# Wide attention of a decoder: one half of every rotated head copied in place, the other half moved by 4 transfers per tile

## The reference

```python
q = split_heads(x @ Wq); k = split_heads(x @ Wk); v = split_heads(x @ Wv)
x1, x2 = (x[..., 0::2], x[..., 1::2])     # apply_rope, on q and k
rot = jnp.stack([x1 * cos - x2 * sin, x1 * sin + x2 * cos], axis=-1)
sim = jnp.einsum('bid,bjd->bij', q, k) * scale
attn = jax.nn.softmax(jnp.where(causal[None], sim, -jnp.inf), axis=-1)
out = jnp.einsum('bij,bjd->bid', attn, v)
return out @ Wo + bo
```

## Time and profile before

| | |
|---|---|
| median of 3 runs | 1898.75 us (1895.04 to 1898.91) |
| profiled execution | 1897.24 us, span 1895.4 us |
| granted TensorE clock, mean | 0.944 of full speed |
| PE busy in the span | 1635.5 us, 86% |
| DVE | 1480.9 us, 78% |
| POOL | 1401.5 us, 74% |
| ACT | 960.2 us, 51% |
| transfers from `wa_rot` to `wa_whole` | 1024 of 64.0 KB |

### The profile page before, as it was taken

How to read it: one execution, slowest core, us unless ns; L and a number is a source line. 1 busy time by engine, 2 the same in 40 slices (tenths; PEclk the granted TensorE clock), 3 DMA queues, 4 the chain that set the end, 5 groups by cost and what they waited for, 6 DMA issues and landing times. The chain is left out here.

```text
span 1895.4 us, 63438 instructions
## 1 busy us (share of the span) xinstructions
PE 1635.5 (86%) x24719; PEld 1351.4 (71%) x24719; DVE 1480.9 (78%) x3166; ACT 960.2 (51%) x2012; POOL 1401.5 (74%) x1249
## 2 busy tenths in 40 slices
PE   4999999999998927489999999999999868918886
PEld 2677777777776826367778778888888657918775
DVE  6888888888887682488899988888888665688765
ACT  3677777777776332344454444444443453125554
POOL 3777778877777545498899888888888635857776
PEclk9999999999999857699999999999999978959999
DMA  8000023000000041344444333343434226552222
GB/s 250 14 7 9 6 73 125 16 18 15 15 16 7 1 134 36 107 117 108 120 119 106 93 96 96 97 97 97 97 97 97 69 73 193 177 164 81 75 76 56
DMA packets 155071, 154.03 MB, mean 81 GB/s; under 512 B 37246, under 2 KB 106944, under 8 KB 154160
## 3 DMA queue, kind: packets, MB, share of 16 engines
q1 hardware_dynamic: 140528, 130.91, 25.6%
q0 software_dynamic: 6704, 15.61, 2.8%
q10 hardware_dynamic: 7696, 5.71, 1.1%
HBM read 58.77 MB, written 26.71 MB: 45 GB/s over the span
## 5 line engine op out<-in xcount | busy, mean ns | idle before, releaser
L1424 POOL TENSOR_TENSOR wa_rot<-wa_rot,wa_cross 128x1024 f32<-128x1024 f32 x128 | 309.1, 2415 | 46.3 <-DVE wa_cross L1636 44.6
L412 POOL TENSOR_TENSOR sa_sd<-sa_sd,sa_mx 128x1024 f32<-128x1024 f32 x128 | 243.3, 1901 | 133.6 <-DVE sa_mx L648 133.6
L592 ACT ACTIVATE sa_sd<-sa_sd 128x1024 f32<-128x1024 f32 x128 | 135.5, 1058 | 115.3 <-POOL sa_sd L412 112.3
L1633 DVE TENSOR_TENSOR wa_rot<-wa_ps_qk,cos 128x1024 f32<-128x1024 f32 x128 | 155.7, 1216 | 42.5 <-PE wa_ps_qk L1490 42.5
L1589 ACT COPY wa_pt<-wa_ps_svt 128x1024 f32<-128x1024 f32 x64 | 64.9, 1014 | 237.3 <-PE wa_ps_svt L1526 237.3
L648 DVE TENSOR_REDUCE sa_mx<-sa_sd 128x16 f32<-128x1024 f32 x128 | 156.1, 1220 | 4.4
L1430 POOL TENSOR_TENSOR wa_sd<-wa_sd,wa_mx 128x1024 f32<-128x1024 f32 x64 | 121.8, 1903 | 50.6 <-DVE wa_mx L1649 50.6
L1490 PE MATMUL wa_ps_qk<-wa_xt,l_wk 128*128 128x128 f32 x1024 | 136.2, 288 | 10.9 <-DVE wa_cross L1636 10.9
L534 PEld LDWEIGHTS sa_ps_o<-sa_vbd,sa_pt 128*64 128x64 f32 x4096 | 130.6, 138 | 19.1 <-issue 10.4
L534 PE MATMUL sa_ps_o<-sa_vbd,sa_pt 128*64 128x18 f32 x4096 | 143.4, 213 | 0.8 <-DVE sa_o L675 0.8
L419 POOL TENSOR_TENSOR sa_km<-sa_k,head_mask 128x512 f32<-128x512 f32 x128 | 135.4, 1058 | 7.3 <-ACT sa_k L583 6.9
(11 more groups left out here) (311 smaller groups left out, 4253.8 us busy)
## 6 DMA issues: line engine op xcount, KB each, us to landing
wa_whole<-wa_rot SPq DMA_DIRECT2D x1024, 64.0 KB, 2.0
choice_dram<-sa_zero_rows SPq DMA_DIRECT2D x32, 256.0 KB, 3.4
choice<-choice_dram SPq DMA_DIRECT2D x32, 256.0 KB, 3.6
x_res<-in_x_dram SPq DMA_DIRECT2D x16, 256.0 KB, 6.6
sa_ctx_t<-in_ctx_t_dram SPq DMA_DIRECT2D x64, 64.0 KB, 1.8
c_index<-in_index_dram SPq DMA_DIRECT2D x2, 2048.0 KB, 7.9
xn_dram<-c_xn SPq DMA_DIRECT2D x16, 256.0 KB, 3.8
cs_ctx_t<-in_ctx_t_dram SPq DMA_DIRECT2D x16, 256.0 KB, 3.0
```

The source lines that it names most:

```text
L412: pool.tensor_tensor(sd[:, v % 4], sd[:, v % 4], mx[:, v % 4].unsqueeze(2).to_broadcast([P, H0, SEQ]), ALU.subtract).then_inc(sub_ready, 1)
L592: act.activation(sd[:, v % 4], sd[:, v % 4], ACT.Exp, scale=scale).then_inc(p_ready, 1)
L1424: pool.tensor_tensor(rot[n][:, v % 2], rot[n][:, v % 2], cross[n][:], ALU.add)\
L1633: dve.tensor_tensor(rot[n][:, v % 2].rearrange("p f j t -> p (f j) t"), src.rearrange("p f j t -> p (f j) t"), bc(k.cos[:], 1, 2 * QUADS), ...
```

## The change

The two halves of a head lie on the same 32 partitions in `rot`. ACT now copies all of `rot[n]` of a tile to `whole[n]`, partition for partition (`copy_rotated`, one instruction of 128x1024 for the queries and one for the keys, lag 2). Half 0 of heads 0 and 2 and half 1 of heads 1 and 3 then lie where they belong. The other half of each head is moved over what the copy put there, by 4 transfers of 64 KB for the queries and 4 for the keys. SP waits for the copy (`copied`) where it waited for `rotated`, and the wait for `s_made`, which protects `whole` of two tiles back, stands ahead of the copy on ACT. The two copies stand in ACT's step on both sides of `x_copy`, the keys' ahead of `weigh`. Heads lie in `whole` in another place (`h // 2` chooses the partitions, `h % 2` the place in the free dimension), and the score matmuls go over heads in the order 0, 2, 1, 3.

```diff
--- before.py
+++ after.py
@@ -1353,6 +1353,7 @@
         qk_made = [sem("q_made"), sem("k_made")]
         crossed = [sem("q_crossed"), sem("k_crossed")]
         rotated = [sem("q_rotated"), sem("k_rotated")]
+        copied = [sem("q_copied"), sem("k_copied")]
         moved = [[sem(f"{m}_moved{n}") for n in range(2)] for m in "qk"]
         mask_made = sem("mask_made")
         v_made, v_ready = sem("v_made"), sem("v_ready")
@@ -1366,7 +1367,7 @@
         own_begun, own_made, own_ready = sem("own_begun"), sem("own_made"), sem("own_ready")
 
         LAST = 5
-        PIECES = 8
+        PIECES = 4
         NG, NEAR, MID = NT // GROUP, 3, 5
 
         def weighed_in(i):
@@ -1398,14 +1399,11 @@
 
             def move(n, t):
 
-                sp.wait_ge(rotated[n], t + 1)
-                if t >= 2:
-                    sp.wait_ge(s_made, t - 1)
+                sp.wait_ge(copied[n], t + 1)
                 for h in range(4):
-                    for half in range(2):
-                        to = h % 2 * D1 + half * ROWS
-                        sp.dma_start(whole[n][to:to + ROWS, t % 2, h // 2], rot[n][h * ROWS:(h + 1) * ROWS, t % 2, half])\
-                          .then_inc(moved[n][t % 2], 16)
+                    to, half = (h ^ 1) * ROWS, 1 - h % 2
+                    sp.dma_start(whole[n][to:to + ROWS, t % 2, h % 2], rot[n][h * ROWS:(h + 1) * ROWS, t % 2, half])\
+                      .then_inc(moved[n][t % 2], 16)
 
             load(k.choice_bufs)
             for t in range(NT):
@@ -1509,12 +1507,12 @@
                 pe.wait_ge(moved[1][v % 2], 16 * PIECES + 8 * PIECES * (t - v % 2))
                 pe.sem_inc(scores_begun, 1)
                 for j in range(QUADS):
-                    for h in (0, 1, 2, 3):
-                        of = slice(h % 2 * D1, (h % 2 + 1) * D1)
+                    for h in (0, 2, 1, 3):
+                        of = slice(h // 2 * D1, (h // 2 + 1) * D1)
                         for b in range(2):
                             rows = slice(b * SEQ, (b + 1) * SEQ)
-                            mm = pe.matmul(scores_ps[rows, h, j * SEQ:(j + 1) * SEQ], whole[0][of, v % 2, h // 2, j, rows],
-                                           whole[1][of, v % 2, h // 2, j, rows], start=True, stop=True)
+                            mm = pe.matmul(scores_ps[rows, h, j * SEQ:(j + 1) * SEQ], whole[0][of, v % 2, h % 2, j, rows],
+                                           whole[1][of, v % 2, h % 2, j, rows], start=True, stop=True)
                 mm.then_inc(s_made, 1)
 
             def p_transpose(i, t, v):
@@ -1572,6 +1570,14 @@
                     act.wait_ge(v_made, t - 3)
                 act.copy(xt[:, v], ps_o[:, 1, 0]).then_inc(xt_ready, 1)
 
+            def copy_rotated(n):
+                def stage(t, v):
+                    act.wait_ge(rotated[n], t + 1)
+                    if late(t, 2):
+                        act.wait_ge(s_made, t - 1)
+                    act.copy(whole[n][:, v % 2], rot[n][:, v % 2]).then_inc(copied[n], 1)
+                return stage
+
             def v_copy(t, v):
                 act.wait_ge(v_made, t + 1)
                 if late(t, 2):
@@ -1611,7 +1617,8 @@
                     act.wait_ge(mid_sems[2], SCALED)
                 if isinstance(i, int) and i == GROUP * (1 + NEAR + MID) - 1:
                     act.wait_ge(far_sems[2], SCALED)
-                for stage, behind in ((o_copy, 5), (v_copy, 3), (normalise, 0), (x_copy, 0), (p_copy, 4), (exponential, 3)):
+                for stage, behind in ((o_copy, 5), (v_copy, 3), (normalise, 0), (copy_rotated(0), 2), (x_copy, 0),
+                                      (copy_rotated(1), 2), (p_copy, 4), (exponential, 3)):
                     if stage is p_copy and isinstance(i, int):
                         for g in weighed_in(i):
                             weigh(g)
```

## The result

| | before | changed |
|---|---|---|
| median | 1895.9 us (20 runs, 1891.97 to 1900.56) | 1899.34 us (20 runs, 1896.38 to 1909.07) |
| ratio to before | | 1.0020, interval 1.0011 to 1.0030 |
| profiled execution, span | 1897.24, 1895.4 us | 1896.38, 1894.4 us |

Forecast were 1895.7 us and 3.1 us less than before; measured are 3.4 us more. Yet the profiled execution of the changed kernel is the shorter of the two. The mean of the five ratios is 1.0009, 1.7 us. That is no difference that can be told from none, and surely not the gain.

A forecast was written before the change was run, and what follows sets the result against it. PE was taken to bound the late steps and SP's backlog of transfer issues the early ones. Saving -9.4 plus copy cost +6.3 gave -3.1 us, from 1898.75 to a median of 1895.7 us, range 1888.5 to 1902.5.

The forecast's parts named there:

- PE sets the pace of the late steps: Late steps of the wide attention: PE busy 99.51 of 100 us, one step 10.78 us, unchanged by the change.
- SP's backlog: Early steps: SP owes 12 us of issues a step of 10.78 to 11.09; with 8 transfers per tile 6.6 us.
- DVE's pace: Steps 7 to 13 without the waits: the pace of steps 17 to 25, 22.18 us a pair, 66.5 for six steps.
- the copy's duration: Each added 128x1024 ACT copy: 1.06 us by the nearest row, 0.96 taken as what it displaces, bounds 0.9 and 1.1.
- the query copy is free: Query copy ahead of the x copy, where ACT waits 1.53 us for PE's transpose: cost nothing.
- the closed chain: Even steps with `weigh`: key copy delays `pair_up` through to PE's key projection, 0.70 us in nine steps, 6.3 us.
- the dearest copy: Upper bound of the key copy's cost in nine steps: 9 x (1.1 + 0.06 - 0.26) = 8.1 us.
- the first term of the sum: Steps 7 to 13: PE's three waits for transfers go, -9.4 us, bounds 11.2 us and nothing.
- Rival E: Nothing seen: DVE takes as long as the waits did and the copy is hidden, 1898.75 us; chance 0.10.
- C: The three waits stay, as something other than SP's issues holds the transfers; copy costs 6.3, 1905 us; chance 0.06.
- D: PE's longer gaps in nine odd steps drop the clock to 1.2 GHz: +12 us, about 1907; chance 0.06.
- F: Key copy waits for POOL at the head of ACT's queue in some steps: +3 us, 1899; chance 0.06.

The follow-up runs named there:

- the five ratios: The changed kernel against before, measured five times: 1.0020, 1.0004, 1.0009, 0.9999 and 1.0012.
- half-moves: Kernel before with 4 of 8 transfers per half and tile, no copies, part of the scores left out: 0.9971 (0.9956 to 0.9986), -5.6 us.
- the fifth: Fifth profile of the unchanged kernel before, run against itself: ratio 1.0010 (0.9993 to 1.0027), steps 7 to 13 in 71.7 us.

## Why the prediction was wrong

**Right:** that PE sets the pace of the late steps (10.78 us before and after); that the waits come from SP's backlog and go with 8 transfers a tile; that DVE's pace, 66.5 us for six steps, lies behind them; the copy's duration; that the query copy is free; that the key copy acts through `weigh`, `pair_up` and the closed chain; and the size of it. The parts in the traces: 68.5 - 66.4 = 2.1 in steps 7 to 13, 139.9 - 136.2 = 3.7 in steps 13 to 25, 0.5 in the rest, together 6.3 us. The first 0.24 of the place in step 6 lies ahead of step 7 and comes on top: 6.5 us, which is nine places of 0.70 and the 0.2 of step 20. (In steps 4 and 5 the copies made the pair shorter, 23.16 us instead of 23.58 in most profiles; why is open.) By the ratios it is 6.6 to 7.4. The 0.70 a place came out as forecast, with the weighing 0.95 later and 0.25 of it hidden by POOL's rotation. Only its place was not: PE stands 0.83 and not 1.05 ahead of the key projection, since 0.24 are paid in the even step, at the output projection. One sum is off without consequence: the dearest copy would give 9 x 0.84 = 7.6 us as the bound and not 8.1, as `pair_up` starts 0.32 and not 0.26 behind the end of the weighing.

**Wrong: the first term of the sum, "I take -9.4 us".** It measured -5.6 us (half-moves; -9.4 lies outside its interval), and 5.2 to 6.3 in four profiles (the 5.2 of the fifth with one stretch at 1.2 GHz in it). The step that failed is the reading of 75.88 us as the transfers' loss. The prediction saw that the clock had fallen behind a wait, and then counted the 3.4 us that two such stretches cost as if every execution had them. It also had a sign that it didn't use: the three waits sum to 7.6 us, and DVE's lateness took part of the same time, so that more than 7.6 could only come from the clock. With -5.6 in the place of -9.4 the sum is +0.7 us, and with the cost by the ratios +1.0 to +1.8: no change that can be told, as the mean of the five ratios has it. Of the 6.5 us between forecast and first measurement, this term explains 3.8.

**Scale.** A net of 3 us was made of two terms of 6 and 9, each of which the profile gave to some tenths in one execution and one of which moved by 4 us between executions (75.9 to 71.7). Rival E (nothing to be seen) was right in effect and wrong in its reason. C and D didn't occur: no wait for `wa_whole` and no stretch at 1.2 GHz between 860 and 1495 us in any of the five profiles of the changed kernel, whose new gaps of PE are 0.83 us. F didn't either, in the steps from 4 on: the key copy follows the x copy at 0.16 us, but for step 20.

**Page and row.** The Trainium skill, "DMA: Bandwidth & Descriptors", section "Anatomy of one DMA", gives about 50 ns for the sequencer's dispatch. The rows disagree as a price of an issue here: in blocks of 32 without a wait between them SP's issues in before are 0.63 to 0.74 us apart (20.2 to 23.6 us a block), and halving their number (and the bytes) ended the waits. The page's figure is for the path through GpSimd.

**Left open.** The first measurement's 1.0020 has an interval that excludes 1.000, and the parts make 0.2 to 1.3 us of its 3.4 by the traces and at most 1.8 by the ratios. What the rest is stays open. Identical code gave 0.9981 with an interval that excludes 1.000 as well, so such an interval does not settle a difference of 0.2%; no run shows a loss of the changed kernel outside the stage, and none excludes one of 1 or 2 us.

## What to carry to other kernels

An instruction put into an engine's idle time is free only if what stands behind it in the queue isn't awaited by a full engine: ask who waits for the next instructions, not only how long the idle time is. Here one place further down in ACT's step was worth some 7 us. And before a loss read from one execution becomes a term of a sum, take the stretches at a lower clock out of it, or read it in a second execution: they come and go.

## What was not expected of the hardware

A late operation also brings others side by side that were apart before, and some of them then take longer. In the timeline of step 20 of the changed kernel, DVE's addition of the experts' outputs to x, both inputs in SBUF, took 1.66 us (1.46 or 1.47 in the others of the nine steps, and 0.68 to 0.76 in the same steps of before):

```profile
1008.57 1.66 DVE L1685 TENSOR_TENSOR x_res<-x_res,choice 128x512 f32<-128x512 f32 x1
```

With the key copy behind the weighing the same instruction took 0.77:

```profile
1006.19 0.77 DVE L1685 TENSOR_TENSOR x_res<-x_res,choice 128x512 f32<-128x512 f32 x1
```

In the changed kernel its first 1.1 us lay beside POOL's subtraction (1007.77 to 1009.67); in the other kernel the subtraction was at its end when it started (1004.52 to 1006.41 against 1006.19), though the rest of it lay beside the start of POOL's rotation (from 1006.38). With the key copy twice it was POOL's subtraction that took 2.36 us instead of 1.90. The Trainium skill, "SBUF — State Buffer", section "Who interferes with whom", says that a DVE instruction with two SBUF inputs contends with a GpSimd instruction that reads SBUF, and that ScalarE never waits on anyone. The rows agree with the first as far as they go: which of two overlapping instructions waits differs from row to row, and no run here took one of them away. For the second, the copies took 1.03 to 1.06 us whatever DVE and POOL did.
